# Pairwise attention pooling: x transposed by VectorE in 32x32 squares instead of by TensorE, three PSUM slots shared by chunks and Gram matrices

## What is computed

```python
row, col = np.triu_indices(F, k=1)          # 741 pairs of fields
ip = x[:, row, :] * x[:, col, :]            # (b, pair, 64)
hidden = relu(einsum('bpd,da->bpa', ip, W_w) + b_w)
logits = einsum('bpa,a->bp', hidden, W_h) + b_h[0]
a = softmax(logits, axis=1)[:, :, None]
y = sum(a * ip, axis=1) @ W_p + b_p         # (b, 1)
```

## Time and profile before

| | us |
|---|---|
| median of 3 runs (lowest, highest) | 1091.17 (1090.26, 1094.05) |
| profiled execution, its own time | 1092.44 |
| span of the profiled execution | 1090.7 |
| TensorE matmuls busy | 1070.5 (98%) |
| VectorE busy | 956.5 (88%) |
| ScalarE busy | 872.2 (80%) |
| GpSimd busy | 865.3 (79%) |
| DMA, mean | 42 GB/s, queue 1 busy 46.1% of 16 engines |
| TensorE's granted clock | 0.996 of full speed |

### The profile page before, as it was taken

One profiled execution on the slowest core, in us unless ns is written; L12 is line 12 of the kernel. 1 busy time (PEld: TensorE's weight loads), 2 busy tenths in 40 slices (PEclk: granted clock), 3 DMA queues, 4 the chain that ended last, 5 costly groups with the idle time before them and its releaser, 6 DMA issues.

```text
span 1090.7 us, 60223 instructions
## 1 busy us (share of the span) xinstructions
PE 1070.5 (98%) x25856; PEld 574.0 (53%) x25856; DVE 956.5 (88%) x484; ACT 872.2 (80%) x884; POOL 865.3 (79%) x327
## 2 busy tenths in 40 slices
PE   7999999999999999999999999999999999999995
PEld 3446555464545646455454555645555464555542
DVE  8798899898998989989998899989989899898991
ACT  5788887888878878888788887878788887887873
POOL 7787887877887877878878878778778788787780
PEclk9999999999999999999999999999999999999998
DMA  3256364443544444462463624627445444534532
GB/s 50 29 43 55 24 59 42 39 46 37 44 45 46 35 45 37 44 58 24 45 55 26 59 36 39 50 29 52 44 37 45 43 38 45 54 27 45 50 23 26
DMA packets 333325, 45.47 MB, mean 42 GB/s; under 512 B 333301, under 2 KB 333301, under 8 KB 333301
## 3 DMA queue, kind: packets, MB, share of 16 engines
q1 hardware_dynamic: 332981, 45.10, 46.1%
q10 hardware_dynamic: 320, 0.07, 0.0%
HBM read 26.59 MB, written 18.54 MB: 41 GB/s over the span
## 4 chain that ended last, share of the span: by engine, by line
PE 97%; DVE 1%; issue 0%; ACT 0%; DMA 0%; ACTq 0%; DVEq 0%
PE z L531 60%; PE logits L551 30%; PE z L489 4%; PE z L472 4%; DVE prod L331 1%; DMA x_rows<-in_r_x_dram 0%; ACT hidden L409 0%; PE logits L541 0%; DVE neg_max L340 0%; DVE weighted L348 0%; ACT exps L432 0%; DVE x_wide L313 0%; DVE exp_bias L342 0%; DVE y_all L354 0%; DVE x_wide L314 0%
## 5 line engine op out<-in xcount | busy, mean ns | idle before, releaser
L409 ACT ACTIVATE hidden<-z,b_col 128x988 f32<-128x988 f32 x768 | 803.4, 1083 | 191.2 <-PE z L531 190.9
L331 DVE TENSOR_TENSOR prod<-x_wide 128x2964 f32<-128x2964 f32 (+1 forms) x257 | 845.6, 3340 | 7.4
L531 PE MATMUL z<-prod,w_tiles 64*32 64x494 f32 x12288 | 770.8, 576 | 2.8 <-issue 2.5
L269 POOL COPY head_w<-head_cols 128x64 f32<-128x64 f32 x252 | 529.3, 2129 | 62.9 <-PE logits L551 62.8
L551 PE MATMUL logits<-hidden,head_w 64*32 64x370 f32 (+1 forms) x8192 | 451.2, 472 | 0.4 <-PE logits L551 0.4
L280 POOL TENSOR_SCALAR x_scaled<-x_wide,wp_col 128x624 f32<-128x624 f32 x64 | 332.8, 5200 | 138.2 <-DVE x_wide L307 132.1
L531 PEld LDWEIGHTS z<-prod,w_tiles 64*32 64x32 f32 x12288 | 284.0, 106 | 235.2 <-issue 144.3
L551 PEld LDWEIGHTS logits<-hidden,head_w 64*32 64x32 f32 x8192 | 203.2, 106 | 213.6 <-issue 197.8
L306 DVE COPY x_wide<-z 128x624 f32<-128x624 f32 x63 | 51.0, 809 | 94.4 <-PE z L472 92.7
L489 PEld LDWEIGHTS z<-x_wide,x_scaled 64*39 64x39 f32 x4096 | 44.9, 113 | 39.7 <-issue 39.7
L489 PE MATMUL z<-x_wide,x_scaled 64*39 64x39 f32 x4096 | 52.4, 202 | 0.8 <-ACT hidden L409 0.8
(11 more groups left out here) (22 smaller groups left out, 26.1 us busy)
## 6 DMA issues: line engine op xcount, KB each, us to landing
x_rows<-in_r_x_dram SPq DMA_DIRECT2D x127, 156.0 KB
gram<-gram_out SPq DMA_DIRECT2D x256, 47.5 KB
gram<-gram_out SPq DMA_DIRECT2D x256, 23.2 KB
values<-gram SPq DMA_DIRECT2D x128, 46.3 KB, 3.5
x_rows<-in_r_x_dram SPq DMA_DIRECT2D x2, 78.0 KB
out_dram<-y_all SPq DMA_DIRECT2D x8, 0.9 KB
w_tiles<-in_L_rec_W_w_dram ACTq DMA_DIRECT2D x4, 16.0 KB, 3.3
head_cols<-in_L_rec_W_h_dram SPq DMA_DIRECT2D x4, 0.2 KB, 2.3
```

Of the source, the lines that this page charges most:

```text
L269: nc.gpsimd.tensor_copy(head_w[:, step % BLOCK_STEPS, :, :], head_cols[:, :, at:at + TILE]).then_inc(head_w_ready, 1)
L331: nc.vector.tensor_tensor(out, one, other, ALU.mult).then_inc(ready, 1)
L409: nc.scalar.activation(hidden[:, i, :, CHUNK * k:CHUNK * (k + 1)], z[:, SLOT[j], :, 0:CHUNK], ACT.Relu, bias=b_col[:, 0:1]).then_inc(z_rea ...
L531: last = nc.tensor.matmul(z[col:col + TILE, SLOT[j], b, 0:CHUNK], w_tiles[row:row + D, col:col + TILE], prod[row:row + D, i, first:first + ...
```

## The change

x is loaded so that a transposition in squares of 32 by 32 yields what is wanted. Partition h x 64 + e x 32 + r of `x_rows` holds, for batch h of each duo and half e of the 64 numbers, field 7 + r (j = 0, 32 rows) and field r (j = 1, 26 rows, the other 6 zeroed once). One VectorE transposition of 1024 elements per partition makes of it `x_wide`: 7, ..., 38, 0, ..., 25, which is 39 fields and the 19 next ones round the circle. Lines of `x_wide` are 64 long now. The load is 8 DMAs of 128-byte rows, waits for the `spread` that reads `x_rows`, and stands behind `write_gram` on SP. TensorE has no transposes but those of block 0, which keeps its buffer `first_x_rows` and its copies. Slots: 13 items a block, in turn.

```diff
+    LINE = 2 * TILE
+    FIRST_FIELD = FIELDS - TILE
+    PIECES = ((FIRST_FIELD, TILE), (0, WIDE - TILE))
...
-    SLOT = (2, 1, 0, 2, 1, 0, 0, 1, 0, 2, 1, 0)
-    EARLIER = (9, 10, 11, 0, 1, 2, 5, "gram", 6, "x", 7, 8)
-    X_SLOT, GRAM_SLOT = 2, 1
+    SLOT = (1, 0, 2, 1, 0, 2, 1, 2, 0, 1, 0, 2)
+    EARLIER = (9, 10, 11, 0, 1, 2, 3, 5, "gram", 6, 8, 7)
+    GRAM_SLOT = 0
...
-    x_rows_dram = x.rearrange("(v u b) f d -> u f v b d", v=BLOCKS, u=2)
+    first_x_dram = x.rearrange("(v u b) f d -> u f v b d", v=BLOCKS, u=2)
+    x_rows_dram = x.rearrange("(v p h) f (e d) -> h e f v p d", v=BLOCKS, h=2, e=2)
...
-        x_rows = sb("x_rows", [ROWS, 2 * ROW_DUOS, D])
-        x_wide = sb("x_wide", [P, BLOCK_DUOS, WIDE])
+        first_x_rows = sb("first_x_rows", [ROWS, 2 * ROW_DUOS, D])
+        x_rows = sb("x_rows", [P, BLOCK_DUOS, 2, TILE])
+        x_wide = sb("x_wide", [P, BLOCK_DUOS, LINE])
...
+        def store_last_y(engine, q):
+            first = y_dram[q, 0:1, 0:1, GROUPS - 1:GROUPS]
+            rows = bass.AP(first.tensor, first.offset, [[1, 2], [2 * QUADS, GROUP_STEPS], [1, 1]])
+            engine.dma_start(rows, y_all[TILE * q:TILE * (q + 1), GROUPS - 1:GROUPS],
+                             allow_slow_non_contiguous=True).then_inc(y_stored, 16)
...
             def load(v):
-                sp.wait_ge(x_cols_ready, v + 2)
-                for u in range(2):
-                    sp.dma_start(x_rows[u * D:u * D + FIELDS, :, :],
-                                 x_rows_dram[u, :, bass.ds(v, 1), :, :]).then_inc(x_loaded, 16)
+                if isinstance(v, int) and v == 1:
+                    sp.wait_ge(x_rows_zeroed, 1)
+                else:
+                    sp.wait_ge(x_spread, v + 1)
+                for h in range(2):
+                    for e in range(2):
+                        for j, (first, rows) in enumerate(PIECES):
+                            at = h * D + e * TILE
+                            sp.dma_start(x_rows[at:at + rows, :, j, :],
+                                         x_rows_dram[h, e, first:first + rows, bass.ds(v, 1), :, :]
+                                         ).then_inc(x_loaded, 16)
...
-                    if not (last and m >= GROUP_BLOCKS - 2):
-                        load(v + 2)
...
                     write_gram(v, m % 2)
+                    if not (last and m >= GROUP_BLOCKS - 2):
+                        load(v + 2)
...
-            sp.dma_start(last_y, y_all[:, GROUPS - 1:GROUPS],
-                         allow_slow_non_contiguous=True).then_inc(y_stored, 16)
+            for q in range(QUADS // 2):
+                store_last_y(sp, q)
...
             nc.vector.memset(head_cols[:, :, :], 0.0).then_inc(zeroed, 1)
+            nc.vector.memset(x_rows[:, :, 1, :], 0.0).then_inc(x_rows_zeroed, 1)
...
             def spread(v):
 
+                dve.wait_ge(x_loaded, 16 * 4 * len(PIECES) * v)
                 dve.wait_ge(prod_ready, BLOCK_STEPS * v)
                 dve.wait_ge(z_ready, ITEMS * (v - 1) + CROSS_AT + 1)
-                dve.wait_ge(x_cols_ready, v + 3)
-                cols = z[:, X_SLOT, :, 0:XCOLS].rearrange("p u (q f) -> p u q f", f=FIELDS)
-                wide = x_wide[:, :, :].rearrange("p (u q) f -> p u q f", u=2)
-                nc.vector.tensor_copy(wide[:, :, :, 0:FIELDS], cols).then_inc(x_spread, 1)
-                nc.vector.tensor_copy(wide[:, :, :, FIELDS:WIDE], cols[:, :, :, 0:OFFSETS]).then_inc(x_spread, 1)
+                nc.vector.transpose(x_wide[:, :, :].rearrange("p q f -> p (q f)"),
+                                    x_rows[:, :, :, :].rearrange("p q j d -> p (q j d)")).then_inc(x_spread, 1)
...
+            act.wait_ge(y_ready, GROUPS)
+            for q in range(QUADS // 2, QUADS):
+                store_last_y(act, q)
...
             def cross_work(v):
 
-                gram_matrices(v, with_x=True)
-                transpose(X_SLOT)
+                assert EARLIER[CROSS_AT] <= BEFORE_GRAM and CROSS_AT % THIRDS == 0
+                gram_matrices(v, prod_of=CROSS_AT // THIRDS)
+                chunk(v, CROSS_AT)
```

More of the change, by code:

```diff
@@ L57, in bass_pairwise_attention_pooling @@
     TILE = 32
+    LINE = 2 * TILE
+    assert D == 2 * TILE and FIELDS >= TILE and WIDE <= LINE
+    FIRST_FIELD = FIELDS - TILE
+    PIECES = ((FIRST_FIELD, TILE), (0, WIDE - TILE))
     assert GROUP_BLOCKS == 4 and GROUPS % 2 == 0
@@ L135, in bass_pairwise_attention_pooling @@
         zeroed = sem("zeroed")
+        x_rows_zeroed = sem("x_rows_zeroed")
         w_loaded = sem("w_loaded")
@@ L205, in _ @@
             for i, (u, batches, _) in enumerate(FIRST_X):
-                sp.dma_start(x_rows[u * D:u * D + FIELDS, batches, :],
-                             x_rows_dram[u, :, 0, batches, :]).then_inc(first_x_loaded[i], 16)
+                sp.dma_start(first_x_rows[u * D:u * D + FIELDS, batches, :],
+                             first_x_dram[u, :, 0, batches, :]).then_inc(first_x_loaded[i], 16)
             for h in range(2):
@@ L272, in scale_x @@
             def scale_x(v):
[L274 removed]
+                pool.wait_ge(x_spread, v + 2)
                 if v == 0:
@@ L462, in _, with transpose, gram_matrices @@
             exponentials(GROUPS - 1, logits[:, :, 0:HCOLS])
+            act.wait_ge(y_ready, GROUPS)
+            for q in range(QUADS // 2, QUADS):
+                store_last_y(act, q)
         @block.tensor
         def _(pe):
-            def transpose(slot, tiles=range(2), duos=range(ROW_DUOS)):
+            def transpose(slot, u, duos):
+                rows = slice(u * D, u * D + FIELDS)
                 for d in duos:
-                    for u in tiles:
-                        rows = slice(u * D, u * D + FIELDS)
-                        duo = x_rows[rows, 2 * d:2 * d + 2, :].rearrange("f h d -> f (h d)")
-                        last = nc.tensor.matmul(z[:, slot, u, FIELDS * d:FIELDS * (d + 1)], duo, ident[rows, :],
-                                                is_transpose=True, start=True, stop=True, tile_position=(u * D, 0))
+                    duo = first_x_rows[rows, 2 * d:2 * d + 2, :].rearrange("f h d -> f (h d)")
+                    last = nc.tensor.matmul(z[:, slot, u, FIELDS * d:FIELDS * (d + 1)], duo, ident[rows, :],
+                                            is_transpose=True, start=True, stop=True, tile_position=(u * D, 0))
                 last.then_inc(x_cols_ready, 1)
-            def gram_matrices(v, with_x=False):
+            def gram_matrices(v, prod_of=None):
                 pe.wait_ge(x_scaled_ready, v + 1)
-                if with_x:
-                    pe.wait_ge(x_loaded, 32 * (v + 1))
+                if prod_of is not None:
+                    pe.wait_ge(prod_ready, BLOCK_STEPS * v + prod_of + 1)
                 before = item(BEFORE_GRAM) if cross_at(v) > BEFORE_GRAM else EARLIER[BEFORE_GRAM]
@@ L517, in claim_slot, with chunk @@
                     pe.wait_ge(act_spread, 4)
-            def hidden_layer(v, j, with_x=True):
+            def chunk(v, j):
                 i, k = j // THIRDS, j % THIRDS
-                if isinstance(v, int) and v == 0 and i == 0:
-                    pe.wait_ge(first_prod_ready if k == 0 else prod_ready, 1)
-                elif k == 0:
-                    pe.wait_ge(prod_ready, BLOCK_STEPS * v + i + 1)
-                claim_slot(v, j, with_x)
-                nc.tensor.sem_inc(z_claimed, 1)
                 for a in range(0, A, TILE):
@@ L535, in hidden_layer, with cross_work @@
                 last.then_inc(z_ready, 1)
+            def hidden_layer(v, j):
+                i, k = j // THIRDS, j % THIRDS
+                if isinstance(v, int) and v == 0 and i == 0:
+                    pe.wait_ge(first_prod_ready if k == 0 else prod_ready, 1)
+                elif k == 0:
+                    pe.wait_ge(prod_ready, BLOCK_STEPS * v + i + 1)
+                claim_slot(v, j)
+                nc.tensor.sem_inc(z_claimed, 1)
+                chunk(v, j)
+            def cross_work(v):
+                assert EARLIER[CROSS_AT] <= BEFORE_GRAM and CROSS_AT % THIRDS == 0
+                gram_matrices(v, prod_of=CROSS_AT // THIRDS)
+                chunk(v, CROSS_AT)
             def open_logits():
@@ L596, in block_work @@
                     cross_work(v + 1)
-                chunks(6, 7)
+                else:
+                    chunks(6)
+                chunks(7)
             pe.wait_ge(ident_ready, 3)
@@ L601, in _ @@
                 pe.wait_ge(first_x_loaded[i], 16)
-                transpose(slot, (u,), range(batches.start // 2, batches.stop // 2))
+                transpose(slot, u, range(batches.start // 2, batches.stop // 2))
             pe.wait_ge(w_loaded, 16 * 4)
@@ L606, in _ @@
             cross_work(0)
-            for j in range(CROSS_AT, HELD):
+            for j in range(CROSS_AT + 1, HELD):
                 hidden_layer(0, j)
```

25 lines of the change are left out of this document (10 added, 15 removed).

## The result

| us | before | changed |
|---|---|---|
| median of the runs (lowest, highest) | 1090.72 (1089.99, 1094.05), 4 runs | 1063.76 (1062.18, 1065.36), 4 runs |
| profiled execution, its span | 1092.44, 1090.7 | 1062.18, 1060.1 |
| ratio, 95% interval | | 0.9747 [0.9722, 0.9772] |

27 us were won, where 44 were forecast; 1063.8 is above the range's end of 1058. So two things are to be told apart: 6 to 7 us by which it is slower than forecast each time, and 10 us that only the first set of runs shows.

The account below looks back on a forecast made before the run. TensorE, busy 98% of the span, was taken as the bound; 39.1 us from transposes and 5.7 from chunk 8's wait, together 44.7, took 1092.44 to 1047.7, stated as 1047 after the median's offset, range 1043 to 1058.

Parts of the forecast that it names:

- the logit bank: TensorE at a group's start: logits copy just in time, costed at nothing; 1.5 us in all if 0.1 late.
- transposes off TensorE, chunk 6 behind Gram: TensorE, each of 63 blocks: 16 matmuls go and chunk 6 follows without a wait, 0.62 us a block, 39.1 us.
- wait of chunk 8: TensorE before chunk 8: its wait for ScalarE's read of chunk 6 goes, 0.09 us a block, 5.7 us in all.
- period: TensorE, one block's Gram start to the next: 15.87 us, down from 16.58 by 0.71.
- T: VectorE's new 32x32 transposition of 1024 elements per partition: taken as 1.2 us, bounds about 0.65 to 2.4.
- VectorE idle before it: VectorE before the transposition: 1 to 1.5 us waiting for Gram matrices; about 1.1 us late after the softmax block.
- VectorE becomes the bound: VectorE's group of four blocks: a slow transposition makes it the bound from T = 2.1 us; no cost below that.
- x late: DMA of x, eight issues behind the Gram writes: lands with 2.7 us of slack before VectorE asks, costing nothing.
- last stores: Kernel's end: four store issues on two queues could save or cost some 0.5 us, taken as nothing.
- the first rival: VectorE bound by a slow transposition: about 1069 us at T = 2.4 (0.10 with mild late x); slower, T over 2.8, 0.04.
- Rival 3: TensorE: transposes partly free, up to 0.2 of 0.71 us a block not won, 1060 us; chance 0.07.
- The packets: DMA of x: 3712 packets a block priced at 20 to 26.4 ns each, 4.6 to 6.1 us a block, costing nothing.

Follow-up runs that it names:

- third profile: Profile of the changed kernel, nothing edited, timed again in a later set of runs beside the kernel before: 1053.91 us, ratio 0.9661.
- e1_swap: Changed kernel with ScalarE's copy of the logits put ahead of its Gram copy at a group's start (the swapped kernel): 1046.76 us, ratio 0.9596.
- second profile: Profile of the changed kernel, nothing edited, in its first repetition beside the kernel before: 1053.34 us, ratio 0.9661.
- e2_oldload: Changed kernel with x loaded as before, 2 DMAs of 39 x 16 rows of 256 bytes, y not the reference's: 1055.49 us, ratio 0.9683.
- e4_tiny8: Changed kernel with its 8 loads of x cut to two rows of fields each, y not the reference's: 1053.19 us, ratio 0.9652.
- first profile: Profile of the changed kernel in its first set of runs, median 1063.76 us; the profiled execution took 1062.18 us.
- e6_loadfirst: Swapped kernel (logits copied first) with SP's load of x put back ahead of the Gram writes: 1046.48 us, ratio 0.9597.
- r2_e1: Second timing of the swapped kernel, the changed kernel with the logits copied ahead of the Gram copy: 1045.49 us, ratio 0.9586.

## Why the prediction was right or wrong

**The step that failed** is the logit bank: "G + 2.3, and TensorE will want the logit bank at G + 2.43 [...] just in time, costed at nothing; if it is 0.1 late it costs 15 x 0.1 = 1.5 us". Both times were right: the copy ended at G + 2.31 (533.26 - 530.95), chunk 7 at G + 2.46. The price was wrong. I compared the end of the copy with the moment at which the array wants the bank, as if the wait stood at the matmul. It stands ahead of the openers and the inner loop, and the 0.84 us between it and the first logit half is sequencer work that must be done before the array runs dry. Before, this took 0.66 us, and 0.75 us of chunk 7 covered it. The change took the 0.6 us of the transposes out from in front of chunk 7 but not from in front of the copy, and left 0.15. So a group's start costs (16.64 - 15.84) - (16.73 - 16.58) = 0.65 us more, 15 x 0.65 = 9.7 us (9.0 by the third profile), not 0 to 1.5. e1_swap takes most of it back, and the same swap in the kernel before opens a gap of the same kind by another wait. This step alone would have left the time within the range. What put the first runs outside it is the 10 us that stay open. The Trainium skill (Perfetto Trace Analysis, Sequencer Loop) describes the parts: instructions for an engine go into its queue, control instructions are carried out by the sequencer; the trace agrees as far as it goes, with the wait as a record of the sequencer's own, and with 0.27 us of "issue" and 0.49 us for the openers' row, as from a queue that had run empty.

The other steps, with what the traces gave:

| step | forecast | measured |
|---|---|---|
| transposes off TensorE, chunk 6 behind Gram | 0.62 us a block | 1.37 - 0.74 = 0.63 |
| wait of chunk 8 | 0.09 | 0.09 |
| period | 15.87 | 15.84, so 63 x 0.74 = 46.6 us |
| T, transposition of 1024 elements | 1.2 (0.65 to 2.4) | 1.246 |
| VectorE idle before it | 1 to 1.5; 1.1 us late after the softmax block | 1.17; idle 0.35 after the softmax block |
| VectorE becomes the bound | from T = 2.1 | 1.9 |
| x late | no, 2.7 us of slack | no wait for x; order on SP free |
| last stores | +-0.5 | none that can be told |
| DMA share | about 0.65 | 0.43 (0.40 in the third profile) |

The sum, by the second profile: 1090.7 - 1050.3 = 40.4 us of span. Of that, 46.6 from the period, -9.7 from the group starts (0.80 - 0.15, fifteen times), 2.8 from the first block (19.60 us from its Gram matrices to the next before, 16.10 now; 3.5 less the 0.7 that is in the period already), the rest 0.7 in small pieces. The first block was in no step; in the third profile it took 18.01, so it is worth 1 to 3 us. Forecast were 44.7. The swapped kernel, in which the failed step is mended, gave 1046.8 and 1045.5, where 1047 had been forecast. That agreement is in part luck: the period gave 1.9 us more than was counted and the first block up to 2.8 that nobody had counted, against (16.11 - 15.84 - 0.15) x 15 = 1.8 that the group starts still cost.

**The rivals.** VectorE and x were no bounds. For T = 2.4 the first rival gave 1069 us; with 2.45 us of transpositions it is 1081, since VectorE's group came to 66.0 us where 65.0 had been counted. Rival 3, a part of the 0.71 us not won, comes nearest to the first runs by its number (1060), but has the wrong place: nothing was lost in a regular block.

**The packets** were too dear in the working, which hid nothing here. At nearly equal spans queue 1 was busy, on the pages of e2_oldload, e4_tiny8 and the third profile of the changed kernel:

```profile
q1 hardware_dynamic: 332913, 45.10, 29.7%
```

```profile
q1 hardware_dynamic: 269787, 27.04, 22.4%
```

```profile
q1 hardware_dynamic: 493815, 54.93, 40.4%
```

The differences to the second give (29.7 - 22.4)% x 16 x 1051 / 63126 = 19 ns for a packet of 256 bytes and (40.4 - 22.4)% x 16 x 1051 / 224028 = 14 ns for one of 128 (16 by the first profile's 43.4%), against 20 to 26 in the prediction. Two of the prediction's three rows were taken where transfers crowd, but the third was of the load alone, at 22.5 ns. Nor does a packet always take the same time: the kernel before moved nearly the same packets (332981) as e2_oldload, and its queue was busy 46.1% of the span, not 29.7%. It has its loads right ahead of the Gram writes; but in the swapped kernel that order gave 41.8% (e6_loadfirst) against 40.6% (r2_e1), so the order alone doesn't explain it. What made the old packets dear is open.

The rule of the 256-byte boundary, which the prediction has from the Trainium skill (DMA: Bandwidth & Descriptors, How a descriptor splits into AXI transactions), would make half of the new packets as dear as the old. 14 against 19 is more than one half, as it would have it, but doesn't show it.

**The 10 us of the first runs** are outside every step. They are no property of the code alone, as two repetitions without them show. They put the measured time outside the range, while the 1053 of the repetitions lies in it.

## What to carry to other kernels

In these kernels a wait ahead of a loop was paid at the sequencer, not at the instruction that needs the data. Ask not "is it met before the engine wants it" but "is there still more work queued on the engine, when it is met, than the instructions and registers behind it take". If a change shortens what stands between a producer and a wait ahead of a loop, move the producer forward too; here a swap of two lines on ScalarE brought 7 to 8 us. Look then at what the swap delays: in the kernel before it cost 4 to 6.5. And run the unedited kernel again with the experiments before an edit gets the credit.

## What was not expected of the hardware

- While two DMAs of 58 rows were under way the sixteen engines were busy 0.15 to 0.17 of the time, and issuing the two took over 11 us; with as many pieces on 64 rows it took 1.92 us. The kernel went from 1054 to 1545 us.
- A wait ahead of a loop on TensorE, met 0.15 us before the array ran dry, exposed 0.78 us of sequencer work at a group's start; a wait for a chunk's slot that was met late, though its matmuls were on time, exposed 0.34 us.
- The same kernel took 1063.8 us in one set of runs and 1053.3 and 1053.9 in two others, the kernel before 1090.7, 1091.4 and 1090.8 beside them. In the trace twelve late blocks stand for 5.5 us of it; in the one that was looked at the word of a semaphore came 1 us late. What holds it up is open.
- The second of two transpositions in a row took 1.20 us, the one that starts after a pause 1.25. By the Trainium skill (Vector Engine (DVE) Microarchitecture Reference, The reshape front-end and per-opcode configuration), one element per cycle and lane, I had estimated 1.07 us plus a start; both agree with it, with 0.13 and 0.18 us for the start.
